# Product-key phase of a four-layer kernel: seven lags with every round written out, two copies moved to ScalarE, and GpSimd's sums as 64 one-input additions

## What is computed

```python
q = (hidden_states @ Wq).reshape(b, t, 2, H, 64)          # H = 4
sim = einsum('btphn,hkpn->pbthk', q, keys)                # 64 keys on each side
sc, ix = top_k(sim, 8)                                    # 8 best of each side
all_sc = (sx[..., :, None] + sy[..., None, :])            # 64 pairs
scores, pk = top_k(all_sc, 8)                             # 8 best pairs, of 1024 experts
w = einsum('btd,bthkd->bthk', hidden_states, down_embed[idx])
w = silu(w) * softmax(scores)
experts_states = einsum('bthk,bthkd->btd', w, up_embed[idx])
mlp = silu(hidden_states @ Wg + bg) * (hidden_states @ Wu + bu) @ Wd + bd
x = x + mlp + experts_states
```

## Time and profile before

| | |
|---|---|
| median of three runs | 2956.55 us |
| the profiled execution, its own time | 2959.04 us |
| span of the profiled execution | 2957.3 us |
| busy: TensorE, VectorE, ScalarE, GpSimd | 84%, 52%, 45%, 33% |
| the product-key phase | 2059.7 to 2481.9 us of the span |
| granted TensorE clock, mean | 0.920 |

### The profile page before, as it was taken

The page is one execution under the profiler, slowest core; times in us unless marked ns, Lnnn a source line. Parts: engine busy times, 40 slices in busy tenths (PEclk is TensorE's granted clock), DMA queues, the critical chain, the costliest instruction groups (busy, mean ns, idle before and its releaser), DMA issues. The chain is left out here.

```text
span 2957.3 us, 55320 instructions
## 1 busy us (share of the span) xinstructions
PE 2472.5 (84%) x16024; PEld 2024.4 (68%) x16024; DVE 1543.0 (52%) x4339; ACT 1323.0 (45%) x3147; POOL 973.2 (33%) x1298
## 2 busy tenths in 40 slices
PE   6899999988797853986899999988699997863895
PEld 3577777767686752983567777767578776762885
DVE  4466666544214345116666666644688885425111
ACT  3466667653231421324656667753344442242221
POOL 0233444411105555545532333311333330544002
PEclk9999999998897976998999999999899998985998
DMA  8121222202564363521122222210100001253684
GB/s 276 57 72 65 85 76 71 86 21 108 196 240 122 111 203 117 178 64 60 52 82 74 64 86 75 65 48 23 60 1 0 0 0 59 85 187 131 240 308 164
DMA packets 150859, 296.59 MB, mean 100 GB/s; under 512 B 25158, under 2 KB 110406, under 8 KB 144560
## 3 DMA queue, kind: packets, MB, share of 16 engines
q1 hardware_dynamic: 138416, 262.92, 26.4%
q0 software_dynamic: 12288, 31.83, 3.5%
HBM read 240.25 MB, written 64.56 MB: 103 GB/s over the span
## 5 line engine op out<-in xcount | busy, mean ns | idle before, releaser
L797 DVE CUSTOM_DVE_ANT_0 prob_l<-ps_l,bias_l,nsn 128x1024 f32<-128x1024 f32 (+3 forms) x256 | 276.7, 1081 | 108.2 <-DVEq L796 62.1
L797 DVE CUSTOM_DVE_ANT_0 cur_sb<-ps_h,bias_s,nsn 128x128 f32<-128x128 f32 (+3 forms) x256 | 139.8, 546 | 238.0 <-DVEq L796 237.8
L725 PE MATMUL ps_l<-khi,stage 128*128 128x512 f32 (+3 forms) x512 | 257.1, 502 | 0.0
L872 ACT ACTIVATE prob_l<-prob_l,nmax 128x1024 f32<-128x1024 f32 (+3 forms) x256 | 252.1, 985 | 2.5 <-DVE nmax L797 2.2
L731 PE MATMUL ps_pt<-ident_sb,prob_l 128*128 128x128 f32 x1664 | 236.7, 277 | 6.1 <-ACT cur_sb L856 2.1
L856 ACT ACTIVATE cur_sb<-ps_pt 128x128 f32<-128x128 f32 (+3 forms) x256 | 110.8, 433 | 264.4 <-PE ps_pt L731 264.4
L690 POOL TENSOR_TENSOR stage<-qo,stage 64x256 fp32r<-64x256 f32 x256 | 198.2, 774 | 47.8 <-POOLq L689 47.8
L731 PEld LDWEIGHTS ps_pt<-ident_sb,prob_l 128*128 128x128 f32 x1664 | 185.8, 141 | 37.0 <-ACT cur_sb L856 15.9
L2271 POOL TENSOR_TENSOR ss<-simx,sim 128x4096 f32<-128x4096 f32 x16 | 113.4, 7085 | 242.6 <-DVE simx L2420 242.6
L681 POOL COPY nsn<-nsn 128x4 f32 (+1 forms) x128 | 25.6, 200 | 505.1 <-DVE diff L814 378.9
L1657 ACT ACTIVATE hT<-ps_h,mlp_ws 128x128 f32<-128x128 f32 x312 | 89.1, 369 | 224.3 <-PE ps_h L1630 224.3
(11 more groups left out here) (338 smaller groups left out, 6102.1 us busy)
## 6 DMA issues: line engine op xcount, KB each, us to landing
mlp_ws<-in_L_ffn_experts_dram SPq DMA_DIRECT2D x39, 2052.0 KB, 7.4
xs<-slot_rows SPq DMA_DIRECT2D x156, 128.0 KB, 2.1
slot_outputs<-ys SPq DMA_DIRECT2D x156, 128.0 KB, 1.9
slot_rows<-zero_sb SPq DMA_DIRECT2D x1, 16384.0 KB, 52.2
bias_l<-in_fside_16xSxS_dram SPq DMA_DIRECT2D x16, 512.0 KB, 3.4
mlp_w<-in_L_ffn_experts_dram SPq DMA_DIRECT2D x8, 1024.0 KB, 7.5
bias_by_partition<-bias_table SPq DMA_DIRECT2D x16, 512.0 KB, 4.1
bias_l<-bias_by_partition SPq DMA_DIRECT2D x16, 512.0 KB, 3.3
```

What stands on the lines that cost most here:

```text
L725: ins = pe.matmul(out, stage[:, b, s, x.h % 2, x.h // 2, :], att[part][:, b * S + lo:b * S + hi], start=False, stop=part == "klo", skip_gr ...
L797: dve.tensor_tensor_reduce(out=spans(x, prob), in0=scored(x), in1=spans(x, bias), scale=-1.0, scalar=nsn[:, b, s, h:h + 1], op0=ALU.add, o ...
L872: act.activation(prob[x.s][:, x.h, 0:x.W], prob[x.s][:, x.h, 0:x.W], ACT.Exp, bias=nmax[:, x.b, x.s, x.h:x.h + 1], scale=-1.0, accum_out=r ...
```

## The change

1. The lags are stretched, 4 to 7 of them (0 to 3 before, 0 to 6 after), and each engine's rounds are written out with `unrolled`. `hidden` of TensorE is split into first_gate_up, last_gate_up and `turned` (the transposes of `gm`, now one round later). `xT` has six buffers, `sim` and `t8` three, `simx` and `hT` two. The semaphores are split by stage.
2. `ps_s` to `sim`, and the second half of `gT`, are copied by ScalarE and no more by VectorE.
3. GpSimd's copy `xs` is gone: TensorE transposes `cur` directly.
4. GpSimd's one `tensor_tensor` of 4096 elements becomes 64 `tensor_scalar` additions of 64 elements each, the added number being a per-partition value of `simx`.
5. The weights are issued in another order. The wait is still for all of them.

```diff
-        sim = ph.sb("sim", [P, 2, HR, NK])
+        sim = ph.sb("sim", [P, 3, 2, HR, NK])
-        simx = ph.sb("simx", [P, HR, NA])
+        simx = ph.sb("simx", [P, 2, HR, NA])
-        hT = ph.sb("hT", [P, NE])
+        hT = ph.sb("hT", [P, 2, NE])
...
             def sums(t, u):
                 gp.wait_ge(dve_a.sem, dve_a.after("simx", t))
                 gp.wait_ge(dve_m.sem, dve_m.after(f"kept{HR - 1}", t - 2))
                 gp.wait_ge(act_e.sem, act_e.after("es", t - 2))
-                gp.tensor_tensor(ss[:, u % 2].rearrange("p h (a b) -> p h a b", b=NK),
-                                 simx[:].unsqueeze(3).to_broadcast([P, HR, NA, NK]),
-                                 sim[:, 1].unsqueeze(2).to_broadcast([P, HR, NA, NK]), ALU.add).then_inc(gp_a.sem, 1)
-            pipeline(gp, NT, 4, (0, stage), (1, sums))
+                for h in range(HR):
+                    for i in range(NA):
+                        ins = gp.tensor_scalar(ss[:, t % 2, h, i * NK:(i + 1) * NK], sim[:, t % 3, 1, h, :],
+                                               simx[:, t % 2, h, i:i + 1], None, ALU.add)
+                ins.then_inc(gp_a.sem, 1)
+            unrolled(gp, NT, 2, (3, sums))
...
             def transposes(t, u):
-                pe.wait_ge(gp_x.sem, gp_x.after("x", t))
                 pe.wait_ge(act_x.sem, act_x.after("xT", t - 1))
                 for k in range(KD):
-                    ins = pe.transpose(ps_x[:, k * P:(k + 1) * P], xs[:, u % 2, k * P:(k + 1) * P], c["ident"][:])
+                    ins = pe.transpose(ps_x[:, k * P:(k + 1) * P], c["cur"][:, t, k * P:(k + 1) * P], c["ident"][:])
...
+            def gate_up(t, u, q):
+                if t == 0 and q == 0:
+                    pe.wait_ge(weights, 16 * len(second))
+                pe.wait_ge(dve_h.sem, dve_h.after(f"h{(q + 2) % 4}", t - 1 if q < 2 else t))
...
+            def turned(t, u):
+                pe.wait_ge(dve_g.sem, dve_g.after("gm", t))
...
-            pipeline(pe, NT, 4, (0, transposes), (3, outputs), (0, queries), (2, retrieval), (0, similarities), (2, hidden))
+            unrolled(pe, NT, 6, (4, first_gate_up), (5, turned), (5, outputs), (4, last_gate_up), (0, transposes), (1, queries),
+                     (4, retrieval), (1, similarities))
...
+            def similarities(t, u):
+                act.wait_ge(pe_s.sem, pe_s.after("sim", t))
+                act.wait_ge(gp_a.sem, gp_a.after("ss", t - 3))
+                act.wait_ge(dve_a.sem, dve_a.after("simx", t - 3))
+                act.activation(sim[:, t % 3].rearrange("p q h n -> p (q h n)"), ps_s[:], ACT.Copy).then_inc(act_s.sem, 1)
...
-                act.activation(gT[:, 0:BANK], ps_w[:, 0:BANK], ACT.Copy).then_inc(act_b.sem, 1)
-            pipeline(act, NT, 4, (0, transposed), (1, exponentials), (0, queries), (2, hidden))
+                act.activation(gT[:], ps_w[:], ACT.Copy).then_inc(act_t.sem, 1)
+            unrolled(act, NT, 6, (4, first_gates), (5, turned), (3, exponentials), (4, last_gates), (0, transposed), (1, queries),
+                     (4, retrieved), (1, similarities))
...
-                dve.wait_ge(gp_a.sem, gp_a.after("ss", t - 1))
-                dve.tensor_copy(sim[:].rearrange("p q h n -> p (q h n)"), ps_s[:]).then_inc(dve_a.sem, 1)
...
+                dve.wait_ge(gp_a.sem, gp_a.after("ss", t - 2))
+                dve.tensor_tensor(simx[:, t % 2], sim[:, t % 3, 0, :, 0:NA], bc(top[:], [P, HR, NA]),
+                                  ALU.subtract).then_inc(dve_a.sem, 1)
...
-                dve.tensor_copy(gT[:, BANK:], ps_w[:, BANK:]).then_inc(dve_b.sem, 1)
...
-            pipeline(dve, NT, 4, (2, all_coefficients), (3, outputs), (2, weighed), (0, search), (2, first_hidden),
-                     (0, search_sums), (2, last_hidden))
+            unrolled(dve, NT, 6, (5, weighed), (6, outputs), (2, search), (4, first_hidden), (2, search_sums), (4, all_coefficients),
+                     (4, last_hidden))
```

More of the change, by code:

```diff
@@ L2224, in product_key_phase @@
         pe_s = ph.steps("sim")
-        dve_a = ph.steps("sim ready s8 top s8x simx cand ready2 t8")
+        act_s = ph.steps("sim")
+        dve_a = ph.steps("s8 top s8x simx cand ready t8")
         gp_a = ph.steps("ss")
@@ new lines, in exponentials, with gate @@
+            def exponentials(t, u):
+                act.wait_ge(dve_a.sem, dve_a.after("t8", t))
+                act.wait_ge(dve_m.sem, dve_m.after("sum8", t - 2))
+                act.activation(e8[:, t % 2], t8[:, t % 3], ACT.Exp).then_inc(act_e.sem, 1)
+                act.wait_ge(gp_a.sem, gp_a.after("ss", t))
+                act.wait_ge(dve_m.sem, dve_m.after(f"kept{HR - 1}", t - 2))
+                act.activation(es[:, t % 2], ss[:, t % 2], ACT.Exp).then_inc(act_e.sem, 1)
+            def gate(t, u, q):
+                if t == 0 and q == 0:
+                    act.wait_ge(weights, 16 * len(second))
+                act.wait_ge(pe_g.sem, pe_g.after(f"gu{q}", t))
+                act.wait_ge(dve_h.sem, dve_h.after(f"h{q}", t - 1))
+                for f in range(2):
+                    fc = 2 * q + f
+                    ins = act.activation(sg[:, fc * P:(fc + 1) * P], ps_gu[:, q % 2, f * P:(f + 1) * P], ACT.Silu,
+                                         bias=bg[:, fc:fc + 1])
+                ins.then_inc(act_g.sem, 1)
@@ new lines, in first_gates, with last_gates, retrieved, turned @@
+            def first_gates(t, u):
+                gate(t, u, 0)
+                gate(t, u, 1)
+            def last_gates(t, u):
+                gate(t, u, 2)
+                gate(t, u, 3)
+            def retrieved(t, u):
+                act.wait_ge(pe_w.sem, pe_w.after("w", t))
+                act.wait_ge(dve_g.sem, dve_g.after("gm", t - 1))
+                act.activation(sw[:], ps_w[:], ACT.Silu).then_inc(act_w.sem, 1)
+            def turned(t, u):
+                act.wait_ge(pe_t.sem, pe_t.after("gT", t))
@@ L2475, in all_coefficients, with hidden @@
                     coefficients(t, u, h)
-            def weighed(t, u):
-                dve.wait_ge(act_b.sem, act_b.after("sw", t))
-                dve.wait_ge(dve_m.sem, dve_m.after("co", t))
-                dve.wait_ge(pe_b.sem, pe_b.after("gT", t - 1))
-                dve.tensor_tensor(gm[:], sw[:], co[:], ALU.mult).then_inc(dve_b.sem, 1)
+            def hidden(t, u, q):
+                if t == 0 and q == 0:
+                    dve.wait_ge(weights, 16 * len(second))
+                dve.wait_ge(act_g.sem, act_g.after(f"sg{q}", t))
+                if q == 0:
+                    dve.wait_ge(pe_y.sem, pe_y.after("y", t - 2))
+                for f in range(2):
+                    fc = 2 * q + f
+                    ins = dve.scalar_tensor_tensor(hT[:, t % 2, fc * P:(fc + 1) * P], ps_gu[:, q % 2, (2 + f) * P:(3 + f) * P],
+                                                   bu[:, fc:fc + 1], sg[:, fc * P:(fc + 1) * P], ALU.add, ALU.mult)
+                ins.then_inc(dve_h.sem, 1)
             def first_hidden(t, u):
-                dve.wait_ge(weights, 16 * len(second))
                 hidden(t, u, 0)
```

139 lines of the change are left out of this document (54 added, 85 removed).

## The result

The kernel after takes 3138.11 us, median of four runs (3136.35 to 3141.61); the kernel before, measured beside it, 2956.78 (2956.48 to 2959.07). The ratio is 1.0613, with a 95% interval of 1.0595 to 1.0631: slower by 181 us. I had predicted 2929.0 us (2916 to 2968) and given slower 0.29.

What follows compares the result with a forecast made beforehand. TensorE (21.7 us), GpSimd (about 21.7) and a two-round loop (21.8) were taken to bound together, at 22.2 us a round. Middle -19.0, start -19.0 and end +10.5 sum to -27.5: 2956.55 becomes 2929.0 us, range 2916 to 2968.

Steps and rivals of the forecast that it cites:

- The step that failed: In GpSimd's sums: a 64-element addition was taken to cost 0.185 us by start-to-start spacing, with ends 0.13 and 0.25.
- wrong in sign: Sign to check, GpSimd's additions away from VectorE's long instructions: spacing 0.185 us; above 0.23 the forecast has the wrong sign.
- The form: GpSimd's round in the middle: 9.9 us of port held by VectorE plus 64 s, giving 21.7 us at s = 0.185.
- The rival that GpSimd becomes the bound: At `sums`, between VectorE's two-input instructions: at s = 0.25 a round of 25.9 us and 2981 us; chance 0.27.
- 16.8 a round: VectorE's busy time in the middle, in us, once the copies and the standing still come off: 234.8 us in 14 rounds.
- added copies: ScalarE's two copies taken over from VectorE: some 0.60 and 0.43 us a round, raising its busy time from 10.9 to 11.9.
- TensorE's floor: TensorE's busy time in the middle: 21.7 us a round, the least a round could take.
- The two-round loop: From a tile's `sums` through `es`, `sw`, `gm` and `kept` to `sums` two tiles later: 20.8 to 21.8 us a round.
- The start: Phase's beginning to tile 1's first gate product: -19 us, bounds -14 and -24, with the first `ss` ending at 2087.3.
- The end: From the last tile's first gate product to the phase's end: 28 us instead of 17.5, a loss of 10.5 us.
- a rival at 0.08: In the middle: the stall goes but something as long replaces it, rounds of 23.75 to 24.6 us, 2951 to 2962; chance 0.08.

## Why the prediction was wrong, point by point

**The step that failed** is the price s of an addition: "The line between them at 64 elements gives 0.185 us; I take it." It is 0.423 us, 2.3 times as much and far outside the bounds of 0.13 and 0.25. It was interpolated from a copy and a select, as the nearest rows in size. The kernel with 64 copies shows that for a copy the line is right (0.181); the error was to take a price by size across a change of operation, and to draw the upper bound from the same two rows. No row of before had GpSimd's `tensor_scalar`, and that should have opened the bound much wider. There was a nearer row, which I did not use, of two-input arithmetic on the same engine (a multiplication in another part of the kernel before):

```profile
L480 POOL TENSOR_TENSOR qn<-raw,rn 128x1024 f32<-128x1024 f32 x16 | 30.4, 1901 | 47.0 <-DVE nsn L448 47.0
```

The line through its 1.90 us and the 7.16 us of `ss` alone gives 0.26 us at 64 elements (an estimate from these two rows). That is what the two-input additions then took, and it is above the 0.23 us at which the prediction calls itself wrong in sign.

The choice between spans and spacings was about 0.055 us. The median span of an addition is 0.443 us and its spacing 0.423, so here either would have told the loss. The rule of the Trainium skill ("Perfetto Trace Analysis", GPSIMD Engine Instruction), which times a GpSimd instruction by the spacing to the next, is not at fault; it decided nothing.

**The form was nearly right.** 9.9 + 64 s with s = 0.423 gives 37.0 us a round; measured 34.97, so the port takes 7.9 us from the additions and not 9.9. With it the sum would have been 14 x (37.0 - 23.56) - 8.5 = +180 us, against +181 (the parts miss in both directions: middle 188 for 157, ends -8.5 for +26; that they nearly cancel is luck). The rival that GpSimd becomes the bound, with `es` waiting for `ss`, TensorE for `qT`, came true in every sign given for it. Its chance of 0.27 was too low, its 2981 us too near.

**VectorE.** "16.8 a round" after the copies and the stall went: 240.08 / 14 = 17.15 us, so the additions cost it 0.4 us a round, not the 1 I took. No `kept` was longer than 1.34 us. Right.

**ScalarE.** 1.03 us a round of added copies was right: (166.36 - 152.00) / 14 = 1.03.

**TensorE's floor** of 21.7 us a round was a little high: two kernels ran at 21.26 in nearly every round.

**The two-round loop** was hidden in the kernel after (GpSimd never idle) and shows only with cheaper additions; with two inputs it is 53 us, 3 more than my form.

**The start** was predicted at -19 us and is +10.8. `ss` ends at 2098.3 in place of 2087.3, which is s again. The rest is a step that I left out: the last two `sg` of tile 0 stand in ScalarE's queue behind the `es` of tile 1 (the row at 2131.94). The coefficients of tile 0 were done at 2124.8, and the gate product still waited until 2140.69. With the copies, at 0.181 us, tile 1's first gate product comes 53.1 us after the phase's beginning, where 56 was forecast; so this step, too, costs only while `es` is late.

**The end** was predicted at 28 us and is 33.1: the coefficients begin 6.6 us in and not 5.1, VectorE then waits 2.07 us for `sw` ahead of `gm`, and the `wd` product takes 5.31 us and not 3.72: the granted clock is 0.82 in the last 9.7 us, after TensorE idled 2.4 us at `gm`, and was 1.00 at the end before.

**Hardly foreseen:** had the sum been left whole, the new order would have brought it against `rest`. The stall of `kept` in the earlier trace rows goes in the new lags, but a worse one takes its place: 6.85 us a round against 1.46. The prediction has this only as a rival at 0.08, without a place, and with rounds of 23.75 to 24.6 us; they were 27.22. Of the kernels with the new lags and the sums whole, only the sixteen pieces and the other order gain clearly.

## What to carry to other kernels

Price an instruction only by rows of the same operation on the same engine; where there are none, the bound must be as wide as the engine's worst operation, and splitting one into 64 multiplies that error by 64. When two engines exclude each other at a port, cut the long instruction only until a piece is about as short as a stall that can be borne (here 16 pieces of 0.59 us: -1.4%), or order the other engine's work so that nothing with two SBUF inputs meets it (-1.2%). Both figures are against the kernel before and hold the moved copies, which alone gave -0.5%. After a change of lags look at which instruction now meets the long one, not only at whether the old stall is gone.

## What the runs showed of the hardware that was not expected

- GpSimd's one-input addition is dearer than its two-input one: 0.423 against 0.261 us at 64 elements, 2.85 against 1.90 us at 1024, 10.6 against 7.16 us at 4096. The per-partition number is 0.09 us of it at 64 elements.
- A two-input instruction on four elements of VectorE took 7.01 us and 8.65 us, in place of 0.16, behind one long GpSimd instruction. The Trainium skill, page "SBUF — State Buffer" (Who interferes with whom), has the rule that a VectorE instruction with two SBUF inputs contends with a GpSimd instruction that reads SBUF, calls the shared port an exclusive lock, and says of VectorE's two-port modes that the first to issue has it for the whole instruction. The two-input sum holds it to its end, to within 0.02 us. The one-input sum doesn't: it let VectorE through 1.7 us before its end, in two kernels.
- Between queued pieces VectorE gets its turn: the `rest` that took 7.01 us behind one sum took 1.86 us with four pieces and 0.57 us with sixteen. With 16 pieces the longest `kept` was 1.47 us, with 64 additions 1.34 us.
